# Quantised feed-forward on one core: two clamps less, and the rounding constant inside the last product

## The reference, cut to what matters

```
def act_qdq(x):                                   # 16 bits, one scale for the whole tensor
    qmax = 2.0 ** 15 - 1.0
    scale = jnp.maximum(jnp.max(jnp.abs(x)) / qmax, 1e-12)
    return jnp.clip(jnp.round(x / scale), -qmax - 1.0, qmax) * scale

x = act_qdq(x)
up = act_qdq(x @ lpbq_dequant(w_up).T)
gate = act_qdq(x @ lpbq_dequant(w_gate).T)
sig = fixed_qdq_u16(jax.nn.sigmoid(gate))
gate = act_qdq(gate * sig)
o = act_qdq(gate * up)
return o @ lpbq_dequant(w_down).T
```

## Time and profile before

| | |
|---|---|
| time, 3 runs | 3478.5 us median, 3477.53 to 3485.69 |
| the profiled execution's own time | 3471.38 us |
| its span, first to last instruction | 3469.6 us |
| mean granted PE clock (1 is full speed) | 0.914 |
| the step `layer1_ffn` in that span | 1999.1 to 2262.6 us, some 263 us |
| busy over the whole span: PE, DVE, ACT | 83%, 58%, 48% |

### The profile page before, as it was taken

The page is one execution under the profiler, slowest core; times in us unless marked ns, Lnnn a source line. Parts: engine busy times, 40 slices in busy tenths (PEclk is TensorE's granted clock), DMA queues, the critical chain, the costliest instruction groups (busy, mean ns, idle before and its releaser), DMA issues. The chain is left out here.

```text
span 3469.6 us, 56019 instructions
## 1 busy us (share of the span) xinstructions
PE 2865.2 (83%) x19677; PEld 2097.6 (60%) x19677; DVE 2018.9 (58%) x5039; ACT 1665.8 (48%) x3702; POOL 543.2 (16%) x530
## 2 busy tenths in 40 slices
PE   6999999999879788488799764466998969996897
PEld 5777777777667567356566531355795545554685
DVE  6777787667569423688666668756012763334223
ACT  6666667666543222366576527233333335554221
POOL 2111011111122232100000000000110013333422
PEclk8999999999989799799899887667998989998898
DMA  3111111111100369200000000061994010001386
GB/s 128 46 38 37 38 46 38 37 38 38 37 23 2 145 210 302 72 2 2 24 11 8 29 0 0 0 103 68 342 344 137 1 53 26 26 26 65 131 275 205
DMA packets 143172, 273.47 MB, mean 79 GB/s; under 512 B 50576, under 2 KB 105104, under 8 KB 138032
## 3 DMA queue, kind: packets, MB, share of 16 engines
q1 hardware_dynamic: 126544, 237.60, 21.4%
q0 software_dynamic: 8688, 23.78, 1.8%
q10 hardware_dynamic: 7664, 8.51, 0.7%
HBM read 222.11 MB, written 47.74 MB: 78 GB/s over the span
## 5 line engine op out<-in xcount | busy, mean ns | idle before, releaser
L3008 ACT ACTIVATE L0a_ex<-bank,L0a_nb 128x128 f32<-128x128 f32 x512 | 145.2, 367 | 120.9 <-PE bank L2937 120.4
L1430 POOL TENSOR_TENSOR L3x_p<-L3x_p,L3x_rsum 128x512 f32<-128x512 f32 x128 | 130.6, 1040 | 415.5 <-DVE L3x_rsum L1501 415.5
L1483 DVE CUSTOM_DVE_ANT_0 L3x_s<-bank,L3x_bias 128x512 f32<-128x512 f32 x128 | 87.0, 681 | 177.7 <-PE bank L1259 177.7
L3274 DVE TENSOR_TENSOR L0a_ru<-bank,L0a_um 128x512 f32<-128x512 f32 x128 | 88.2, 689 | 170.8 <-PE bank L2929 156.3
L3265 DVE SCALAR_TENSOR_TENSOR L0a_xf<-L0a_xc,L0a_conv,L0a_xf 128x256 f32<-128x256 f32 x432 | 178.4, 480 | 9.3 <-ACT L0a_xf L3070 7.8
L3186 POOL TENSOR_TENSOR L0a_sum_sq<-L0a_sum_sq,L0a_sq 128x512 f32<-128x512 f32 x56 | 74.5, 1331 | 692.6 <-ACT L0a_sq L3105 692.6
L2851 PE MATMUL bank<-x_feat,L0a_wx 128*128 128x256 f32 x576 | 138.5, 392 | 4.1 <-ACT L0a_xc L3057 4.1
L2937 PE MATMUL bank<-L0a_ru,L0a_vm 128*128 128x512 f32 x256 | 134.2, 606 | 0.0
L2894 PE MATMUL bank<-x_feat,L0a_wz 128*128 128x256 f32 x512 | 119.5, 383 | 9.4 <-DVE L0a_yacc L3365 6.2
L1483 DVE CUSTOM_DVE_ANT_0 L1x_s<-bank,L1x_bias 128x256 f32<-128x256 f32 x256 | 92.9, 419 | 56.3 <-PE bank L1259 41.1
L2851 PEld LDWEIGHTS bank<-x_feat,L0a_wx 128*128 128x128 f32 x576 | 108.9, 195 | 25.4 <-issue 7.0
(11 more groups left out here) (707 smaller groups left out, 7514.2 us busy)
## 6 DMA issues: line engine op xcount, KB each, us to landing
L2f_wt<-in_L2f_w SPq DMA_DIRECT2D x23, 2180.0 KB, 9.2
L0f_wt<-in_L0f_w SPq DMA_DIRECT2D x39, 898.0 KB, 6.2
L3f_wt<-in_L3f_w SPq DMA_DIRECT2D x39, 768.0 KB, 5.5
L0a_wx<-in_L0a_wx SPq DMA_DIRECT2D x72, 256.0 KB, 3.1
L0a_wz<-in_L0a_wz SPq DMA_DIRECT2D x32, 512.0 KB, 4.3
L2a_band<-conv_taps SPq DMA_DIRECT2D x4, 2048.0 KB, 22.0
context_keys_values<-L2f_zeros ACTq DMA_DIRECT2D x32, 256.0 KB, 4.3
L0f_xs<-rows_by_expert SPq DMA_DIRECT2D x39, 128.5 KB, 3.3
```

Source lines behind the costliest of these rows:

```text
L1430: nc.gpsimd.tensor_tensor(p_, p_, rsum[g // n % 2][:, g % n, :].to_broadcast([P, NK]), ALU.mult).then_inc(sig("divided"), 1)
L1483: ins = vec.tensor_tensor_reduce(out=s[:, at:at + nk], in0=bank[:, at:at + nk], in1=bias[r % 2][:, e, :], scale=-scale, scalar=3e38, op0=A ...
L3008: last = a(ex[g % 3][:, j, b * P:(b + 1) * P], bank[:, at:at + P], ACT.Exp, bias=nb[r % 2][:, b, h:h + 1])
L3274: rv.empty(vec.tensor_tensor(ru[g % 2][:], bank[:].rearrange("p (j t) -> p j t", j=2), um[:].unsqueeze(1).to_broadcast([P, 2, T]), ALU.mult))
```

## The change

`clip` loses its lower bound (L1782) everywhere it is called in this step, so it is one DVE instruction where it was two. In the product loop the gate is not clipped at all: the `clip` ahead of L1980 goes, and L1980 takes off `ROUND` in its first operation where it took the maximum with -32768. The lower bound, and for the gate in the product loop the upper bound too, are thereby no longer computed; both are ruled out by the scales. The dequantisation of the weights and the sigmoid's rounding (L1929, L1930) stay as they are. No wait, semaphore, buffer or DMA changes.

```
-        def clip(ch, vec, a, low=True):
+        def clip(ch, vec, a):
 
             ch.link(vec.tensor_scalar(a, a, -ROUND, QMAX, ALU.add, ALU.min))
-            if low:
-                ch.link(vec.tensor_scalar(a, a, -QMAX - 1.0, None, ALU.max))
...
                     dve.wait_ge(sig("mix_rounded"), m + 1)
-                    clip(ch, vec, gate[:, m, :], low=False)
-                    ch.link(vec.scalar_tensor_tensor(out=gate[:, m, :], in0=gate[:, m, :], scalar=-QMAX - 1.0, in1=up[:, m, :],
-                                                     op0=ALU.max, op1=ALU.mult))
+                    ch.link(vec.scalar_tensor_tensor(out=gate[:, m, :], in0=gate[:, m, :], scalar=-ROUND, in1=up[:, m, :],
+                                                     op0=ALU.add, op1=ALU.mult))
                     ch.link(absmax(mx[:, 1, m:m + 1], gate[:, m, :]))
```

## The result

The changed kernel took 3454.9 us in the median of six runs (3442.36 to 3456.04) against 3478.65 us before (3476.48 to 3485.69); the ratio is 0.9921, 95% interval 0.9904 to 0.9938. The medians lie 23.8 us apart and the means 27.5 us, which is what the ratio says. The forecast was 3455.5 us.

What follows compares the result with a forecast made beforehand. DVE was taken to bound most of the gate loop and all of the product loop, PE the gate products and output. Savings 0.6 + 6.3 + 15.1 + 1.0 = 23.0 us took 3478.5 to 3455.5 us, range 3447 to 3465.

Steps and rivals of the forecast that it cites:

- nothing for the merge: Product loop: L1980 with an add first stays at 2293 ns; rival that it is dearer, 3463.1 us, chance 0.06.
- 5 x 1.26: Gate loop: five of six removed L1782 lie on DVE's path, 6.3 us saved; the first is hidden.
- 12 x 1.26: Scales and product loop: 6 L1782 on `up` and 6 L1780 on the gate, each on the path, 15.1 us saved.
- Nine of the 28 instructions: Second L1782 on x, the gate loop's first and seven in the output: hidden by waits or PE's work, worth nothing.
- The cover of 0.14 us ahead of the mix scale: Between the scales: ACT's 1.40 us idle covers the 1.26 us saved on `up` chunk 0, with 0.14 to spare.
- the tightest place: Gate loop, second round: ACT's sigmoid rounding ends 0.3 us before DVE would come for it, so the gain is whole.
- ACT would idle near 1.3 us a round: Gate loop: ACT's idle time falls from 2.55 to near 1.3 us a round, so DVE remains the bound.
- The 8.50 us of the forecast: Gate loop: ACT's need per round, its 11.05 us round less 2.55 us of idle time.
- Input, 0.6 us: Input: PE starts 0.6 us sooner, not 1.26, because ACT's copy is late next; bounds 0.3 and 1.3 us.
- Output, 1.0 us: Output: only the first of eight L1782 is ahead of PE's start, 0.99 us; seven are hidden by PE's work.
- the low level's cost: Output: PE's product starts at clock 0.50; first result after 8.37 us, next 5.17 us later, so 3.2 us lost.
- a clock that changes behind the step: Later steps: PE's clock shifts with the earlier start, up to 12 us either way, 3443.5 to 3467.5 us; chance 0.15.

Runs made afterwards that it cites:

- the merge alone: Kernel before with only L1780 ahead of the product removed and ROUND taken off inside the product, all L1782 kept; scales and product loop 55.42 us against 63.00.
- the other parts alone: Kernel before with L1782 removed from x, the gate loop and the output, product loop unchanged; ratio 0.9977 (0.9960 to 0.9994) to the kernel before.

## Why the prediction was right

The mechanism was right in the gate loop, the product loop and the output: which instructions lie on the path, and what each costs. At the input it is shown for PE's start only. That the median agrees with the forecast to 0.6 us was luck, for the whole kernel's gain came out at 27 us by the first timing's ratio and at 17 us by the second's.

**Prices.** 1.26 us for a clamp on 128x2048 and nothing for the merge: the gate loop gave 6.30 us for 5 x 1.26, the product part 15.14 us for 12 x 1.26, the merge alone 7.58 us for 6 x 1.26. The rule "Don't try to fuse for perf" of the Trainium skill ("VectorE: DVE Perf Modes", Rules for kernel authors), read to say that a merge gains nothing, didn't hold: merging took a whole instruction away and cost nothing (2292 ns for the merged one). The second half of its line, fewer operations, did.

**Covers.** Nine of the 28 instructions were priced at nothing, and the kernel that has them back shows no loss. The cover of 0.14 us ahead of the mix scale held too; ACT's bracket is gone. So did the tightest place, in the gate loop's second round: ACT's rounding of the sigmoid ends at 2098.29 and DVE comes for it at 2098.63, without a wait; 0.3 us was forecast.

**Engines next in line.** Right that DVE stays the bound in both loops. I said that ACT would idle near 1.3 us a round; it had no steady round at all, but caught up until the fifth, and its own round is 8.21 us. The 8.50 us of the forecast was the round less its waits and so 0.3 us too long; the error was harmless because it went the safe way.

**Input, 0.6 us.** This is the weak term. PE's first unit did start 17.45 us behind the step's first DVE instruction in place of 18.01, held by ACT's copy as forecast. But the third maximum, which lets the next dequantisation start, came at 25.18 us in one profile of the changed kernel and 25.85 us in the other, and at 25.73 us in the first profile before, 26.12 us in the second. The input part spans 85.41 to 86.55 us in the eight kernels without the clamp ahead of PE's start and without extra products there, 85.81 to 86.69 us in the four with it; the means, 86.1 and 86.3, are 0.15 us apart. So the start is shown, the gain at the end of the part is not. The agreement to 0.1 us in the first pair of profiles was luck.

**Output, 1.0 us.** Right for the start (0.99 us). The further 0.71 us is the clock, and nothing shows it to be of the change's making: the kernels that keep all eight L1782 here have 43.36, 43.62, 44.58 and 44.65 us, those without the first 43.29 to 44.28 us. The prediction put the low level's cost at 8.37 - 5.17 = 3.2 us; against the 41.68 us of a product that starts at the full level it was 2.9 us, since even there the first result takes 5.45 us. By the rule cited in the prediction ("TensorE: Matmul & The Clock Gate", Part 1, of the Trainium skill), that the check runs freely, a low stretch of changing length is to be expected; the rows agree with it, and no run here shows the check itself.

**The rest of the program.** From the start of the next step on, the 1205 us stayed between 1197 and 1209 us in all profiles, in no order, so the rival of a clock that changes behind the step came to nothing in the changed kernel (1204.4 and 1206.7 us). Ahead of the step, where all these kernels are alike, its start lies anywhere between 1996.55 and 2012.03 us. Both spreads are as large as the effects that whole kernels are asked for. They can account for the two timings of the same changed kernel, 0.9921 and 0.9952 or 27 and 17 us, around a step that is some 23 us shorter; that they do is not shown, and in the second timing it was the kernel before that had moved (median 3472.7 us for 3478.65; the changed kernel's was 3457.1 us, for 3454.9).

Part of the variation ahead of the step is PE's clock in the router of layer 0. From its first product (L504) to the next step's (L418) it takes 16.71 us in nine profiles, at a mean granted clock of 0.50, 13.59 us in three, at 0.63, and 10.76 us in two, at 0.80. That is up to 6 of the 15.5 us; no run tried extra products there. The router's own start lies between 1165.73 and 1176.33 us, and what makes that vary wasn't sought.

## What to carry to other kernels

An instruction taken off a busy engine is worth its duration plus its gap where no bracket follows it in the timeline, and nothing where one does: sort the removed instructions by that before adding them up, and read each part's other engine for its own round, not for the time between its waits. Cut the step at instructions that both kernels have: where their program was the same, the two loops agreed to 0.13 us from execution to execution, while whole runs of one kernel, timed together, spread over 8 to 24 us. Where an engine's first work after a long idle time is on the path, look at its clock there; work of no use ahead of it bought 1.6 to 3.0 us at the output and 2.7 to 4.0 us at the input, and cost 0.7 us where it came too late.

## What the runs showed of the hardware

The clock's rise at PE's start isn't at a fixed distance from it: the low level lasted 5.9 us from the start of the output's product in the first profile before and 4.4 us in the first of the changed kernel, and the product's 192 records took 43.29 to 44.65 us with the low level at its start and 41.60 to 41.68 us without. PE's turnings (products with the identity) ran at the high level once the clock was up, 0.88 us for six records in place of 1.54. They can raise it too: in the profile of the other parts alone PE sat idle for 15.54 us, then did nothing but turnings from 1167.17 us on (L498), and the granted clock, 0.50 between 1168.60 and 1169.60, had a mean of 0.67 up to 1170.40 and was 1.00 behind that, while the next other product (L504) began only at 1170.48.
